# Turning the layout of a DRAM bounce buffer and of the tile it fills: query/key rows for head attention

## The reference

```python
def _attn(x, W_qkv, b_qkv, W_ao, b_ao):
    b, s, d = x.shape
    qkv = jnp.einsum('bsd,od->bso', x, W_qkv) + b_qkv
    qkv = qkv.reshape(b, s, 3, H, DH)
    q = jnp.moveaxis(qkv[:, :, 0], 2, 1)
    k = jnp.moveaxis(qkv[:, :, 1], 2, 1)
    v = jnp.moveaxis(qkv[:, :, 2], 2, 1)
    scores = jnp.einsum('bhqd,bhkd->bhqk', q, k) * SCALE
    wts = jax.nn.softmax(scores, axis=-1)
    o = jnp.einsum('bhqk,bhkd->bhqd', wts, v)
    o = jnp.moveaxis(o, 1, 2).reshape(b, s, d)
    return jnp.einsum('bsd,od->bso', o, W_ao) + b_ao

def _forward(x, ...):
    for l in range(L):                                   # L = 4
        m = _mamba(x, ...);  x = _ln(x + m, g1[l], be1[l])
        a = _attn(x, W_qkv[l], b_qkv[l], W_ao[l], b_ao[l])
        x = _ln(x + a, g2[l], be2[l])
        h = jax.nn.gelu(jnp.einsum('bsd,fd->bsf', x, W_f1[l]) + b_f1[l], approximate=False)
        x = x + jnp.einsum('bsf,df->bsd', h, W_f2[l]) + b_f2[l]
    return x
```

## Time and profile before

| | us |
|---|---|
| median of 3 runs | 3244.02 (3241.69 to 3244.47) |
| the profiled execution | 3241.69, its span 3240.0 |
| PE busy | 2796.0 (86%) |
| DVE busy | 1868.7 (58%) |
| ACT busy | 1770.4 (55%) |
| POOL busy | 801.9 (25%) |
| mean granted TensorE clock | 0.94 of full speed |

### The profile page before, as it was taken

One profiled execution on the slowest core, in us unless ns is written; L12 is line 12 of the kernel. 1 busy time (PEld: TensorE's weight loads), 2 busy tenths in 40 slices (PEclk: granted clock), 3 DMA queues, 4 the chain that ended last, 5 costly groups with the idle time before them and its releaser, 6 DMA issues.

```text
span 3240.0 us, 56618 instructions
## 1 busy us (share of the span) xinstructions
PE 2796.0 (86%) x17396; PEld 1730.6 (53%) x17396; DVE 1868.7 (58%) x3116; ACT 1770.4 (55%) x2669; POOL 801.9 (25%) x864
## 2 busy tenths in 40 slices
PE   6877799787899777898878979999966999799999
PEld 4444446444455444464444546666644777466666
DVE  5567635577445677445676354544446787454444
ACT  6457656377655477653676554444422666544444
POOL 0212100122101222102221024444540000244444
PEclk8989999799899799998799989999987999899999
DMA  2133200233100333001232000000003332000000
GB/s 95 47 101 99 80 6 8 79 108 100 41 13 8 103 106 107 8 8 61 87 109 71 5 7 1 0 0 0 0 0 107 98 96 69 2 4 6 3 6 6
DMA packets 70250, 150.49 MB, mean 46 GB/s; under 512 B 10080, under 2 KB 29024, under 8 KB 69856
## 3 DMA queue, kind: packets, MB, share of 16 engines
q1 hardware_dynamic: 70112, 148.76, 15.2%
HBM read 79.00 MB, written 67.11 MB: 45 GB/s over the span
## 4 chain that ended last, share of the span: by engine, by line
PE 43%; issue 24%; DVE 14%; POOL 10%; DMA 4%; ACT 2%; DVEq 1%; SPq 1%; POOLq 1%; ACTq 0%
DVE hmx L1848 11%; POOL hhlo L2178 9%; PE ps L947 8%; PE ps L753 3%; PE ps L972 2%; PE ps L716 2%; PE ps L680 2%; PE ps L686 2%; PE ps L792 2%; PE ps L828 2%; PE ps L1153 2%; PE ps L814 1%; DMA hqk<-hqk_scratch 1%; DMA hqk_scratch<-hqks 1%; PE ps L1154 1%
## 5 line engine op out<-in xcount | busy, mean ns | idle before, releaser
L1848 DVE TENSOR_REDUCE hmx<-ps 128x2 f32<-128x512 f32 x1024 | 660.2, 687 | 281.4 <-PE ps L947 281.4
L1444 ACT ACTIVATE hpt<-ps 128x1024 f32<-128x1024 f32 x512 | 522.0, 1023 | 279.7 <-PE ps L959 277.8
L2178 POOL TENSOR_TENSOR hhlo<-hh,hhh 128x512 fp32r<-128x512 f32 x320 | 412.8, 1290 | 464.8 <-ACT hhh L1523 463.8
L947 PE MATMUL ps<-hqk 24*128 24x256 f32 x2048 | 307.0, 357 | 221.5 <-DVE hmx L1848 199.5
L1518 ACT ACTIVATE sil<-ps 128x512 f32<-128x512 f32 x320 | 190.8, 596 | 441.9 <-PE ps L1155 437.9
L947 PEld LDWEIGHTS ps<-hqk 24*128 24x128 f32 x2048 | 190.2, 204 | 445.9 <-DVE hmx L1848 418.8
L1942 DVE TENSOR_TENSOR su<-ps,sil 128x512 f32<-128x512 f32 x256 | 177.1, 692 | 326.6 <-PE ps L1155 318.4
L972 PE MATMUL ps<-hpt,hvx 128*32 128x256 f32 x4096 | 294.3, 408 | 2.0 <-ACT hpt L1444 1.6
L959 PE MATMUL ps<-hqk 26*128 26x256 f32 x2048 | 271.0, 347 | 1.7 <-ACT hpt L1444 1.4
L1523 ACT ACTIVATE hhh<-hh 128x512 fp32r<-128x512 f32 x320 | 199.5, 623 | 40.9 <-DVE hh L1945 26.9
L2135 POOL CAST hqks<-hqk 128x512 fp32r<-128x512 f32 x64 | 40.4, 631 | 650.5 <-ACT hqk L1424 629.5
(11 more groups left out here) (247 smaller groups left out, 5579.9 us busy)
## 6 DMA issues: line engine op xcount, KB each, us to landing
hqk_scratch<-hqks SPq DMA_DIRECT2D x64, 768.0 KB, 3.2
hqk<-hqk_scratch SPq DMA_DIRECT2D x256, 192.0 KB
qk_scratch<-qks SPq DMA_DIRECT2D x16, 768.0 KB, 3.3
k<-qk_scratch SPq DMA_DIRECT2D x16, 384.0 KB
qv<-qk_scratch SPq DMA_DIRECT2D x64, 96.0 KB
mw<-mw_in SPq DMA_DIRECT2D x10, 516.5 KB, 4.2
w12raw<-w_in SPq DMA_DIRECT2D x1, 2560.0 KB, 9.6
streams<-x_in SPq DMA_DIRECT2D x8, 256.0 KB, 5.5
```

The lines of the kernel that those rows point to most:

```text
L947: return mm(ps[:, o % 2, qt * SEQ:(qt + 1) * SEQ], hqk[r][32 * g:32 * g + 24, j, 0, qt * P:(qt + 1) * P], hqk[r][32 * g:32 * g + 24, j, 1, ...
L1444: A(hpt[:, j, g:g + 2, :, :], ps[:, 2 + g:4 + g, :], ACT.Exp, scale=QSCALE).then_inc(hd_exp, 1)
L1848: V.tensor_reduce(hmx[:, r, :, 4 * g + j], ps[:, o % 2, :].rearrange("p (t k) -> p t k", t=2), AX.X, ALU.max).then_inc(hd_max, 1)
L2178: G_.tensor_tensor(hhlo[:, k % 4, :], hh[:, k % 2, :], hhh[:, k % 4, :].bitcast(F32), ALU.subtract).then_inc(e_lo, 1)
```

## The change

The axes j and a change places in the tiles `hqk` (partition, then a, j, n in place of j, a, n), and `hqk_scratch` gets the order g, d, t, a, j, n in place of j, g, d, t, a, n. For a row (g, d, t) everything that goes into one partition of `hqk` now lies in one run of 8 KB in DRAM, where it was four runs of 2 KB. In return a partition of `hqks` is no longer one run of 6 KB in DRAM: it is six runs of 1 KB, 4 KB apart. The spill is written as four DMAs, one for each j, each from 32 partitions of `hqks`; `hd_spill` counts 64 for a sequence in place of 16. The matmuls, the memset of the keys' rows and `send_max` only name other addresses of the same tiles.

```diff
-        hqk = [at(f"hqk{r}", [P, 4, 2, SEQ], F32R, where=w) for r in range(4)]
+        hqk = [at(f"hqk{r}", [P, 2, 4, SEQ], F32R, where=w) for r in range(4)]
...
-        hqk_d = nc.dram_tensor("hqk_scratch", (4, GROUPS, DH, 3, 2, SEQ), F32, kind="Internal").ap()
+        hqk_d = nc.dram_tensor("hqk_scratch", (4, DH, 3, 2, 4, SEQ), F32, kind="Internal").ap()
...
-        hd_spill = counter("hd_spill", 16)
+        hd_spill = counter("hd_spill", 64)
...
                     sp.wait_ge(hd_parts, nth(hd_parts, B))
                     sp.wait_ge(hd_scat, every(hd_scat, B - 1))
-                    sp.dma_start(hqk_d.rearrange("j g d t a n -> (j g d) (t a n)"),
-                                 hqks[:].bitcast(F32).rearrange("p t a n -> p (t a n)")).then_inc(hd_spill, 16)
+                    rows = hqk_d.rearrange("g d t a j n -> j (g d) (t a) n")
+                    for j in range(4):
+                        sp.dma_start(rows[j], hqks[32 * j:32 * j + 32].bitcast(F32).rearrange("p t a n -> p (t a) n"))\
+                          .then_inc(hd_spill, 16)
...
-                    rows = hqk_d.rearrange("j g d t a n -> g (d t) j (a n)")
+                    rows = hqk_d.rearrange("g d t a j n -> g (d t) a j n")
                     for g in range(GROUPS):
-                        sp.dma_start(hqk[r][32 * g:32 * g + 24].bitcast(F32).rearrange("p j a n -> p j (a n)"), rows[g])\
-                          .then_inc(hd_scat, 16)
+                        sp.dma_start(hqk[r][32 * g:32 * g + 24].bitcast(F32), rows[g]).then_inc(hd_scat, 16)
...
-                        sp.dma_start(hqk[r][24 + part:P:32, :, 0].bitcast(F32),
+                        sp.dma_start(hqk[r][24 + part:P:32, 0].bitcast(F32),
                                      hmt[16 * part:16 * part + 16].bitcast(F32)).then_inc(hd_mx, 16)
...
-                              hqk[r][32 * g:32 * g + 24, j, 0, qt * P:(qt + 1) * P],
-                              hqk[r][32 * g:32 * g + 24, j, 1, :], start=True, stop=True)
+                              hqk[r][32 * g:32 * g + 24, 0, j, qt * P:(qt + 1) * P],
+                              hqk[r][32 * g:32 * g + 24, 1, j, :], start=True, stop=True)
...
-                              hqk[r][32 * g:32 * g + 26, j, 1, kt * P:(kt + 1) * P],
-                              hqk[r][32 * g:32 * g + 26, j, 0, :], start=True, stop=True)
+                              hqk[r][32 * g:32 * g + 26, 1, j, kt * P:(kt + 1) * P],
+                              hqk[r][32 * g:32 * g + 26, 0, j, :], start=True, stop=True)
...
-                    G_.memset(hqk[r][:, :, 1].bitcast(F32), 1.0)
+                    G_.memset(hqk[r][:, 1].bitcast(F32), 1.0)
```

## The result

| | before | with the change |
|---|---|---|
| median | 3249.43 us (3241.57 to 3257.42, 9 runs) | 3267.37 us (3254.77 to 3280.04, 9 runs) |
| ratio | | 1.0058, 95% interval 1.0038 to 1.0079 |
| profiled execution | 3241.69 us, span 3240.0 | 3267.46 us, span 3265.8 |
| granted TensorE clock, mean | 0.940 | 0.933 |

The change made the kernel 0.58% slower; 0.55% was forecast. The medians are of runs taken together. The median of before is 5.4 us above that of the first three runs, so the ratio and not the absolute time is what answers to the forecast. One further execution of the changed kernel took 11,876 us, for a reason that no row shows; it is in neither the median nor the ratio. Lines from L554 on have moved by one or two numbers.

What follows compares the result with a forecast made beforehand. DVE's row maxima and PE's matmuls bound most; the transfers count only at layers' starts. Layers 1 to 3 lose 4.3 us each (12.9), layer 4 5.0: 3244.0 + 17.9 = 3262 us, 0.55% slower, range 3244 to 3280.

Steps and rivals of the forecast that it cites:

- Place: Start of each layer's head attention: the transfers matter only there, 17.9 us in sum; later steps add nothing.
- The spill's term: Spill at a layer's start: 32 partitions per DMA give 218 GB/s, 3.6 us of data, 1.8 us more.
- the further issues: Spill's three added DMA issues, 0.34 us each: cost nothing of their own, as earlier data still lasts.
- The second spill: Layers 1 to 3, one engine about 2 us late: 0.7 us more, between 0.5 and 1 us.
- The scatter: Keeps 24 partitions per DMA, reads grow from 2 to 8 KB: no gain, data still at about 164 GB/s.
- the second rival: Scatter held by gathered reads, freed by 8 KB runs: 17 us faster, 3227 us; chance 0.11.
- Reads of few partitions: Spill's reads from SBUF: limited like writes, 218 GB/s with 32 partitions.
- the first rival: Reads of few partitions not limited: spill 0.5 us more, 5 us in all, 3249 us; chance 0.19.
- Late maxima in each step: Rival: spill read at 163 GB/s, PE waits 0.4 us in each of 52 steps; 3297 us; chance 0.13.
- The 0.7 us of room: Later steps: maxima landed by about 298.8, PE wants them at 299.55, so the longer spill stays hidden.

## Why the prediction was right

- **Place.** The waits and the chain at the layers' starts carried it. With two tensors in turn the spills stay as dear, and the change costs about 6 us in place of 18, as much as the starts grow there (5.9 us). So the later steps do not carry it.
- **The spill's term**, 1.8 us forecast: 1.9 measured for the first (3.19 to 5.13), 1.8 for the third. Its make-up was a little off. The few partitions cost 1.3 us (by the columns as measure) to 1.45 us (by one DMA) and not 1.8: at 201 to 205 GB/s where two DMAs share a half and more at the seam in the middle, 3.5 us of data and not 3.6, against 2.0 and not 1.8 before. The other 0.5 us come from the issue. The prediction had the further issues free at 0.34 us. They cost 0.61 us in the new form, and while the three further ones are indeed nearly free (0.15 us by columns), the first, at 0.67, holds back the first byte. The two errors cancelled, which is luck.
- **The second spill**, 0.7 us forecast in layers 1 to 3: on average nothing (5.64, 5.01 and 5.28 us after, 5.46, 5.51 and 5.36 before). In layer 4 it took 5.8 us in place of 3.2, 2.6 more, because there, too, an engine was now late, and in layer 2 none was. So layers 1 to 3 lost 3.5, 4.4 and 3.8 us, not 4.3 each, and layer 4 lost 6.7 and not 5.0. The sum hid this as well: which layers have the late engine varies from kernel to kernel (last section), and without layer 4's the starts would have lost nearer 16 us than 18.5.
- **The scatter**, no gain forecast: in the same stretch of it the rate is 194 GB/s for 196. Its first landing in layer 1 took 0.3 us less, most others between 0.15 us less and 0.3 us more, and layer 2's first 0.9 us longer (7.64 for 6.74), which is part of that layer's 4.4. Runs of 8 KB don't free it, and the second rival is out. That the 24 partitions hold it is also what the order of the halves points to: the same pieces, in another order of the partitions, landed 0.3 to 0.6 us sooner in each layer's first scatter.
- **Reads of few partitions**: limited like writes, at 201 and 205 GB/s with 32 partitions. The Trainium skill ("SBUF — State Buffer", section "Door 1: The DMA port swizzle") gives 189 GB/s for 32 partitions at 1 MiB and about 218 without the fixed costs, and now this case's reads agree as well. So the first rival is out. The same page's section "Can I just issue two DMAs to hit both halves?" has two DMAs to different halves gain only 6% over one. Over a whole transfer this case is near that: the order of the halves brought the spill only 0.15 us of 5.1, and each layer's first scatter 0.3 to 0.6 us of 6.7. At the seam itself the two overlap by more, 266 GB/s for 205.
- **Late maxima in each step**: six of the 52 steps had them, 0.5 to 1.3 us long and 4.6 us together, where the rival had all of them and the forecast none. Some of it is made up later: from the first step to the end of a layer's head attention the change needs 265.4 to 267.1 us, before it was 264.8 to 265.4, 3.3 us more in all four. An example in layer 3:

```profile
1169.43 3.46 SPq L556 DMA_DIRECT2D hqk_scratch<-hqks  x4
1172.93 1.21 SPq L571 DMA_DIRECT2D hqk<-hmt  x2
```

```profile
1176.03 0.38 PE L948 MATMUL ps<-hqk 24*128 24x256 f32 x2 [1.33 <-DMA hqk<-hmt]
```

The four issues took 3.46 us there in place of 2.57, and the maxima's DMAs went out right behind them. A 16 KB transfer of instructions was on one of the DMA engines at that moment, as in the two other steps that were over 0.7 us late; the three that were 0.5 us late had none. That it is the cause is read from the trace, and no run tested it. The 0.7 us of room that the prediction gave was a little less: in the median step the maxima now land 5.6 us after the spill's issue, 5.3 before, and 0.55 us ahead of PE's step. That is enough for most steps and not for these. With two tensors in turn the changed kernel has 12 late steps, 8.9 us together, and yet loses no more than its starts do, so a late step costs less than its wait.

## What to carry to other kernels

When a layout is turned so that one side of a bounce through DRAM gets long runs, count the partitions that each DMA touches on the other side before the length of its runs: splitting a 128-partition transfer of 768 KB by partitions cost 1.45 us, splitting it by columns 0.15, and runs of 8 KB in place of 2 gained next to nothing. A transfer with a share of 1% on the chain can be worth 0.6% when it stands in a serial stretch, here three times in turn with another; look there for what makes it serial, since a second buffer and another order of four DMAs gained 0.4%.

## What the runs showed of the hardware

- The cost of an issue depends on how its two sides are described. About 0.4 us when both have the same shape (32 x 1536, or 32 x 6 x 256), 0.56 to 0.67 when one is 192 x 1 x 256 and the other 32 x 6 x 256, and 0.65 to 0.83 for the scatter when its source became 8 x 3 x 2048 against 24 rows. The first byte comes later with it: no data for 0.7 us after the first issue in the one case, 1.15 us and more in the other.
- One late DMA engine of the sixteen made the second spill take 5.4 to 5.5 us in three layers of the kernel before and 3.2 in the fourth, and which layers have it changes from kernel to kernel. The traces tell when. Near each second spill, 16 KB of instructions are moved on one of the same engines. In layer 1 of the kernel before this falls into the spill (150.03 to 155.49 us), in layer 4 ahead of it (here 1521.50 to 1522.90; from 1522.93 to 1526.12 there is none). These are the lines of that queue in the two stretches:

```profile
q8 instruction: 1, 0.02, 1.9%
...
q8 instruction: 1, 0.02, 5.4%
```

| layer | before: transfer starts, from the spill's issue | before: spill lands after | change: transfer starts | change: spill lands after |
|---|---|---|---|---|
| 1 | +1.1 us | 5.46 us | +1.9 us | 5.64 us |
| 2 | +1.0 | 5.51 | -2.7 | 5.01 |
| 3 | +1.0 | 5.36 | +0.9 | 5.28 |
| 4 | -1.2 | 3.19 | +1.0 | 5.83 |

In the seven kernels with one DRAM tensor, 28 second spills in all, it is the same. Five had the transfer start ahead of their issue, and they landed after 3.2 to 5.0 us, as fast as the undisturbed spills of their kernel. The other 23 had it 0.4 to 1.9 us behind the issue, and each landed 0.2 to 2.3 us late. In layer 2 with the change it fell into the first scatter, the one that took 7.64 us; in the four others of the five it fell there too and cost 0.2 us at most. No run moved this transfer, so that it makes the engine late is read from the traces and not tested.
